# Last state space layer: decay sums from running sums in three bfloat16 parts, one product per unit

## What is computed

```python
def segsum(x):
    """x: (..., T) -> (..., T, T); out[..., i, j] = sum_{j<k<=i} x[..., k]; -inf above diag."""
    ...
def ssd_chunk_scan(X, dA, Bm, Cm, chunk):
    ...
    A = jnp.transpose(dA.reshape(b, c, chunk, h), (0, 3, 1, 2))
    A_cum = jnp.cumsum(A, axis=-1)
    Lm = jnp.exp(segsum(A))
    Y_diag = jnp.einsum('bcshn,bczhn,bhcsz,bczhp->bcshp', Cm, Bm, Lm, X)
...
dt = jax.nn.softplus(A_log)
x_in = x / dt[..., None]
y_ssm = ssd_chunk_scan(x_in * dt[..., None], -dt, Bm, Cm, CHUNK)
```

## Time and profile before

| | us |
|---|---|
| median of 3 runs | 1528.91 |
| lowest and highest | 1528.41 to 1533.25 |
| the profiled execution, its own time | 1531.77 |
| its span, first to last instruction | 1530.0 |
| block `l3a` in it, first `ln` transpose to the last residual | about 1211 to 1434 |
| scan of g = 0, first `cb` to last `o` | about 1266 to 1329 |
| scan of g = 1 | about 1366 to 1433 |

### The profile page before, as it was taken

How to read it: one execution, slowest core, us unless ns; L and a number is a source line. 1 busy time by engine, 2 the same in 40 slices (tenths; PEclk the granted TensorE clock), 3 DMA queues, 4 the chain that set the end, 5 groups by cost and what they waited for, 6 DMA issues and landing times.

```text
span 1530.0 us, 25564 instructions
## 1 busy us (share of the span) xinstructions
PE 1384.1 (90%) x9742; PEld 865.6 (57%) x9760; DVE 912.6 (60%) x1665; ACT 766.3 (50%) x1847; POOL 456.7 (30%) x400
## 2 busy tenths in 40 slices
PE   7869999999899879999999998898997789889799
PEld 3434556555466545666667773665664545545536
DVE  7784322224578654555556688854787587676631
ACT  3452111111777566777776446457776545363230
POOL 3230000000000168786882000120742435314200
PEclk9979999999999999999999999998998898987989
DMA  8020221001200300000000100020001100000000
GB/s 256 28 83 1 67 59 34 1 0 73 92 2 2 125 0 8 7 8 8 8 7 1 76 23 1 1 83 1 2 2 72 56 0 3 3 1 3 30 0 28
DMA packets 21854, 48.12 MB, mean 31 GB/s; under 512 B 1506, under 2 KB 16995, under 8 KB 20580
## 3 DMA queue, kind: packets, MB, share of 16 engines
q1 hardware_dynamic: 21732, 46.47, 8.7%
HBM read 41.22 MB, written 5.24 MB: 30 GB/s over the span
## 4 chain that ended last, share of the span: by engine, by line
PE 68%; DVE 18%; ACT 6%; issue 4%; POOL 4%; DMA 0%; DVEq 0%; ACTq 0%; POOLq 0%
PE PS L862 49%; PE PS L1094 5%; DVE work L2568 5%; PE PS L1153 3%; PE PS L959 3%; PE PS L863 3%; ACT work L1697 2%; PE PS L876 2%; PE PS L1191 2%; DVE small L2040 1%; DVE work L2186 1%; DVE X L2547 1%; DVE work L2536 1%; POOL work L795 1%; PE PS L864 0%
## 5 line engine op out<-in xcount | busy, mean ns | idle before, releaser
L862 PE MATMUL PS<-XT,WB 128*128 128x512 f32 (+1 forms) x688 | 300.5, 595 | 5.1 <-DVE XT L2066 2.8
L862 PEld LDWEIGHTS PS<-XT,WB 128*128 128x128 f32 (+1 forms) x688 | 127.1, 191 | 149.7 <-issue 145.8
L1697 ACT ACTIVATE work<-PS,small 128x128 f32<-128x128 f32 x512 | 137.2, 415 | 45.9 <-DVE small L2371 45.8
L2261 DVE TENSOR_TENSOR work<-PS,work 128x512 f32<-128x512 f32 x48 | 33.1, 691 | 170.1 <-PE PS L862 170.1
L1625 ACT ACTIVATE work<-PS 128x512 f32<-128x512 f32 x48 | 28.7, 597 | 194.6 <-PE PS L862 194.6
L647 POOL TENSOR_SCALAR small<-small 128x4 f32<-128x4 f32 x22 | 5.0, 229 | 402.2 <-DVE small L2043 402.1
L2371 DVE TENSOR_REDUCE small<-PS 128x4 f32<-128x512 f32 x128 | 80.4, 684 | 41.4 <-PE PS L862 40.1
L862 PE MATMUL PS<-XT,WA 128*128 128x512 f32 (+2 forms) x224 | 98.4, 615 | 4.8 <-DVEq L2571 2.5
L2568 DVE SCALAR_TENSOR_TENSOR work<-PS,vec,work 128x508 f32<-128x508 f32 (+2 forms) x108 | 80.2, 742 | 14.3 <-DVE work L2568 7.2
L1094 PE MATMUL PS<-WB,work 128*128 128x256 f32 x384 | 86.9, 379 | 0.5 <-DVE work L2266 0.5
L1094 PEld LDWEIGHTS PS<-WB,work 128*128 128x128 f32 x384 | 72.8, 190 | 18.3 <-issue 7.7
(11 more groups left out here) (377 smaller groups left out, 2860.2 us busy)
## 6 DMA issues: line engine op xcount, KB each, us to landing
WB<-in_l0f SPq DMA_DIRECT2D x8, 768.0 KB, 7.6
WB<-in_l1x SPq DMA_DIRECT2D x1, 6144.0 KB, 19.2
WB<-in_l0f SPq DMA_DIRECT2D x32, 96.0 KB, 6.8
WB<-in_l2f SPq DMA_DIRECT2D x1, 3072.0 KB, 10.2
WA<-in_l3a SPq DMA_DIRECT2D x1, 2624.0 KB, 8.9
WB<-in_l3f SPq DMA_DIRECT2D x1, 2064.0 KB, 7.6
WA<-in_l1f SPq DMA_DIRECT2D x1, 2056.0 KB, 10.0
C<-in_ctx SPq DMA_DIRECT2D x2, 1024.0 KB, 7.0
```

What stands on the lines that cost most here:

```text
L862: mm = lambda o, l, r, s, e: nc.tensor.matmul(o, l, r, start=s, stop=e)
L1697: f(wk(12288 + (u % 8) * G + h * P, P), bank(j)[:, h * P:(h + 1) * P], ACT.Exp, bias=sm(704 + (u % 8) * 4 + h, 1)).then_inc(*act_step(*([j ...
L2261: v.tensor_tensor(l0f_h(m)[:, lo:lo + G], bank(j), l0f_s(m)[:, lo:lo + G], ALU.mult).then_inc(*dve_step(j))
```

## The change

The sums are now taken as differences of running sums. For token i and source j of one head the sum is cum(i) minus cum(j), where cum is the running sum of the steps inside the half. cum is float32; it is split into three bfloat16 parts whose sum is exact, and the difference is one product in bfloat16.

- The `plans()` list gets two new jobs `cum` behind `c` 8 of g = 0. They hold their banks until the third part has been taken.
- TensorE makes cum with 16 small products (`running_sums`), and twice subtracts a part from it (`without_part`), behind `c` 10 and behind `z` 1. ScalarE takes the parts (`split_sums`): after the SiLU of channels 7 and 9, and after the gate of `z` 1, all in g = 0.
- SyncE writes the parts to DRAM (`cum_park`, 6 DMAs) and, for each of the 16 quads, reads them back in 6 DMAs: three of 8 partitions x 4 x 128 elements into the left operand (rows 64 to 87), three of 2 partitions x 32 x 64 elements into the right operand (rows 88 to 93). There are two sets of buffers. The set for quad n is loaded once the last unit of quad n-2 is done.
- The other rows of the two operands are constants: GpSimd writes an identity and a pattern in the block `l2a`, and a pattern after `ln`; VectorE writes the masked rows (`later_tokens`, two instructions of 64 x 2048), one before the copy of `dt` and one after it.
- `seg` is now one bfloat16 product for a unit, 94 rows deep, 128 x 512. GpSimd's 64 tiles (L841) and their waits are gone.
- VectorE waits for the DRAM writes ahead of the fifth unit's scores, and makes two small patterns (32 x 8 and 32 x 2) at the kernel's start.

The core of the diff:

```diff
-        l += [("c", cc, g) for cc in range(12)] + [("z", 4 * g + i) for i in range(4)] + [("ea", g)] + \
+        l += [("c", cc, g) for cc in range(9)] + ([("cum", 0), ("cum", 1)] if g == 0 else []) + \
+            [("c", cc, g) for cc in range(9, 12)] + [("z", 4 * g + i) for i in range(4)] + [("ea", g)] + \
...
+            sp.wait_ge(cum_parts, 6)
+            for g in range(2):
+                for part in range(3):
+                    sp.dma_start(cum_park[part, 4 * g:4 * g + 4].rearrange("b h f z -> h b f z"), cum_part(part)[:, 4 * g:4 * g + 4]).then_inc(cum_parked[g], 16)
+            for n in range(16):
+                b, h0, into = n // 2, 32 * (n % 2), decay_in[n % 2]
+                if n % 8 == 0:
+                    sp.wait_ge(cum_parked[n // 8], 48)
+                if n < 2:
+                    sp.wait_ge(decay_rows, n + 3)
+                    sp.wait_ge(masked_rows, n + 1)
+                else:
+                    sp.wait_ge(*full(J("l3a", "seg", (n - 2) // 8, (n - 2) % 8 * 4 + 3)))
+                for part in range(3):
+                    sp.dma_start(decay_left(...)...).then_inc(into, 16)
+                    sp.dma_start(decay_right(...)...).then_inc(into, 16)
...
-                for u in range(32):
-                    n = 32 * g + u
-                    if n >= 4:
-                        pool.wait_ge(*full(job_of["l3a", "seg", (n - 4) // 32, (n - 4) % 32]))
-                    steps = dt_exchanged[:, n * 8:n * 8 + 8] if n % 2 else wk(14336 + n * 8, 8)
-                    nc.gpsimd.tensor_tensor(r3(l3a_step(n), 64), steps.unsqueeze(2).to_broadcast([P, 8, 64]),
-                                            tri_halves.unsqueeze(1).to_broadcast([P, 8, 64]), ALU.mult).then_inc(half_steps.sem, half_steps.give())
...
+                    if (g, cc) == (0, 8):
+                        running = running_sums()
+                    if (g, cc) == (0, 10):
+                        without_part(running, 0)
...
+                    if (g, cc) == (0, 1):
+                        without_part(running, 1)
...
-                        pair = [(u, begin("l3a", "seg", g, u)) for u in (2 * t, 2 * t + 1)]
-                        for u, o in pair:
-                            pe.wait_ge(half_steps.sem, half_steps.next())
-                            for lo in (0, 64):
-                                at = 64 - lo if u % 2 else lo
-                                ins = mm(o[at:at + 64, :], cst("strict", lo, lo + 64)[:, lo:lo + 64], l3a_step(32 * g + u)[lo:lo + 64, :], True, True)
-                            end(ins, "l3a", "seg", g, u)
+                        for u in (2 * t, 2 * t + 1):
+                            n = 8 * g + u // 4
+                            o = begin("l3a", "seg", g, u)
+                            if u % 4 == 0:
+                                pe.wait_ge(decay_in[n % 2], 96 * (n // 2 + 1))
+                            end(mm(o, decay_left(u % 8)[0:94, :], decay_right(u % 8)[0:94, :], True, True))
...
+            def split_sums(part):
+                for half in range(2):
+                    j = J("l3a", "cum", half)
...
+                    f(cum_part(part)[:, :, half, :], r3(bank(j, 64), 64), ACT.Copy, scale=-1.0).then_inc(cum_parts, 1)
+                    if part == 2:
+                        act.wait_ge(cum_parts, 5 + half)
+                        act.sem_inc(bank_free[bank_of[j]], 1)
...
+                    if g == 0 and cc in (8, 10):
+                        split_sums(cc // 2 - 4)
...
+                    if (g, cc) == (0, 1):
+                        split_sums(2)
```

More of the change, by code:

```diff
@@ L263, in build @@
         identb, causalb, onesb = sb("identb", P, BF16), sb("causalb", 4 * P, BF16), sb("onesb", P, BF16)
-        small = sb("small", 848)
+        small, pattern = sb("small", 848), sb("pattern", 16)
         WORK = 18432
@@ L820, in _ @@
             roots()
-            pool.wait_ge(halves_ready, 2)
-            pool.wait_ge(steps_ready, 1)
[L823 to L827, removed]
+            pool.wait_ge(*full(job_of["l3a", "ln", 1, 1]))
+            for slot in (0, 4):
+                nc.gpsimd.tensor_copy(decay_right(slot, 4)[64:96, :].rearrange("p (u h z) -> p u h z", h=8, z=64),
+                                      by_head.unsqueeze(1).unsqueeze(3).to_broadcast([32, 4, 8, 64])).then_inc(decay_rows, 1)
+                pool.wait_ge(decay_rows, 3 + slot // 4)
+            pool.wait_ge(steps_ready, 1)
             for i in range(4):
@@ L1369, in _, with running_sums, without_part @@
             end(ins)
+            def running_sums():
+                pe.wait_ge(steps_ready, 1)
+                sums = [begin("l3a", "cum", half) for half in range(2)]
+                for half, o in enumerate(sums):
+                    lo = 64 * half
+                    for b in range(NB):
+                        ins = nc.tensor.matmul(o[0:64, b * 64:b * 64 + 64], wk(14336 + b * 64, 64, lo, lo + 64), cst("tri", lo, lo + 64)[:, lo:lo + 64],
+                                               start=b == 0, stop=True, skip_group_check=True)
+                    ins.then_inc(cum_sums, 1)
+                return sums
+            def without_part(sums, part):
+                for half, o in enumerate(sums):
+                    pe.wait_ge(cum_parts, 2 * part + half + 1)
+                    ins = more(r3(o[0:64, :], 64), identb[0:64, 0:64], cum_part(part)[:, :, half, :], True)
+                    if part:
+                        end(ins, "l3a", "cum", half)
+                    else:
+                        ins.then_inc(cum_sums, 1)
             for g in range(2):
@@ L1954, in _ @@
             hidden_evac(6)
+            def split_sums(part):
+                for half in range(2):
+                    j = J("l3a", "cum", half)
+                    if part < 2:
+                        act.wait_ge(cum_sums, 2 * part + half + 1)
+                    else:
+                        act.wait_ge(*full(j))
+                    f(cum_part(part)[:, :, half, :], r3(bank(j, 64), 64), ACT.Copy, scale=-1.0).then_inc(cum_parts, 1)
+                    if part == 2:
+                        act.wait_ge(cum_parts, 5 + half)
+                        act.sem_inc(bank_free[bank_of[j]], 1)
             ln("l3a")
@@ L2096, in masks_and_ones @@
                 v.tensor_copy(onesb[:, :], cst("ones")).then_inc(*dve_step())
+                v.tensor_reduce(by_head, cst("ident", 64, 96).rearrange("p (a c) -> p c a", c=8), AX.X, ALU.add).then_inc(patterns, 1)
+                v.tensor_reduce(by_half, cst("ident", 64, 96).rearrange("p (a c) -> p c a", c=2), AX.X, ALU.add).then_inc(patterns, 1)
                 for i in range(4):
@@ L2686, in _, with later_tokens @@
             raw, dt, rx = wk(13312, 512), wk(14336, 512), wk(14848, 512)
+            def later_tokens(slot):
+                v.tensor_scalar(r3(decay_right(slot, 4)[0:64, :], 64), cst("strict", 0, 64)[:, 0:64].unsqueeze(1).to_broadcast([64, 32, 64]),
+                                NEG, None, ALU.mult).then_inc(masked_rows, 1)
+            later_tokens(0)
             j = J("l3a", "dt")
@@ L2728, in scores @@
                         dve.wait_ge(*full(J("l3a", "yb", g, (u - 8) // 4)))
+                    if (g, u) == (0, 4):
+                        for i in range(2):
+                            dve.wait_ge(cum_parked[i], 48)
                     cbm = l3a_cbm(u % 2)[:, (u % 8 // 2) * 64:(u % 8 // 2 + 1) * 64]
```

35 lines of the change are left out of this document (26 added, 9 removed).

## The result

| | before | after |
|---|---|---|
| median of the runs (20 each), us | 1528.94 | 1532.69 |
| lowest to highest | 1522.86 to 1533.63 | 1528.70 to 1540.51 |
| span of the profiled execution | 1530.0 | 1529.4 |
| ratio, with its 95% interval | | 1.003 (1.0016 to 1.0044) |

What follows compares the result with a forecast made beforehand. VectorE was taken to pace the convolutions, a ScalarE-TensorE-VectorE chain the scan's head, TensorE with waits the scan. Terms -9.2 - 1.3 + 7.8 + 0.3 + 3.0 = +0.6 on 1528.91 gave 1529.5 us, no change; range 1517 to 1546.

Steps and rivals of the forecast that it cites:

- Part 3: Head of the g = 0 scan: `cum` jobs hold two banks, delaying `z` 3, `ea`, `eb` and `x`; +7.8 us.
- rival A: TensorE's low clock stays through the head of the scan: +12.9 to +17 us for +7.8, 1535 to 1539; chance 0.22.
- Part 2: Before each scan: without GpSimd's tiles, VectorE's L2719 falls from 1.95 to 1.3 us; -1.3 us in all.
- Part 1: Scan: shorter `seg` saves TensorE 1.05 us a quad at full clock, partly lost to waits; -9.2 us in all.
- the second quad is free: Octets 2 and 3 of each g: second quad's `seg` saving counts fully, 1.2 us an octet, -4.8 us together.
- Part 4: First octet of g = 0: TensorE idles after the shorter `seg`, so the scan begins at the low clock; +3 us.
- Part 5: DMAs: the parts' writes and each quad's six reads from DRAM stay hidden, by 3 us for later quads; 0.
- rival B: Scan: DRAM reads come late because two-partition copies use few engines; +10 to +25 us, 1540 to 1555; chance 0.13.
- the copies: ScalarE: six copies of 0.6 us each; the first four delay a first tap by at most 0.3 us; +0.3 us.
- Rival C: Scan follows TensorE more than thought: saving 14 to 17 us, 1518 to 1523; chance 0.27 including lesser savings beyond 4.6 us.

Runs made afterwards that it cites:

- e2: Kernel before plus only the running sums, their two banks and the three parts, with no reads and the old `seg`: ratio 1.0047 to before, +7.2 us.
- e1: Changed kernel with all three parts taken one step earlier, so that the `cum` banks are free sooner: ratio 0.9967 to before, median 1525.73 us.
- e3: Changed kernel with each 94-row `seg` product made twice: ratio 1.0039 to before, 1.4 us over after by the ratios.
- e7: Kernel before with only the residual's addition of the output product moved ahead of the C-B products on VectorE: ratio 0.9902 to before.
- e10: e7 with the old `seg` made twice for the last 24 units of each g: ratio 1.0022 to before.
- e12: Kernel before with the whole old `seg` made three times for the first quad of octets 2 and 3 of each g: ratio 1.0033, +5.0 us.
- e8: e1 with the residual added early and the `seg` products of each g's first eight units made three times: ratio 0.9874 to before, 1509.55 us.
- e9: e8 with the `seg` products of the other 48 units made twice: ratio 0.9926 to before.

## Why the prediction came out as it did

The forecast, no change, was right at its edge: +4.6 us measured (2.4 to 6.7) for +0.6, and since the interval leaves out zero, "slightly slower" describes it as well. The mechanisms were mostly as written. One term was mis-sized, the saving in the scan.

- **Part 3 was right.** +7.8 us for the held banks; the rows show +7.3, e2 alone +7.2 us (3.5 to 10.9), and e1 takes it away again. The chain was as counted: gates, copy, `z` 3, `ea`, two `eb` (3.78 for 3.94), `x` (3.58 for 3.68). The clock came back after the pause (0.94 from 1260 to 1265), so that rival A was not so. The masked rows were hidden as counted; they took 2.27 and 1.22 us where I had 2.8 each.
- **Part 2 was right**: L2799 takes 1.23 us in both g instead of 1.95 and 2.05 (1.3 forecast).
- **Part 1, the wait, was right; the sum of it was too large.** The third `y` waits 2.58, 2.58, 2.58 and 2.93 us where 2.7 was forecast, and octet 2 of g = 0 is 1.11 us shorter (1.2 forecast). But the same octet of g = 1 is only 0.18 shorter (17.10 to 16.92). The step that failed is "the second quad is free: 1.05 us at full clock, 2.3 where it was low". I priced the rest of the octet as unchanged, while the wait grew by 0.9 us and what stands behind a longer wait runs at the lower clock longer: the small products 2.05 us against 1.77 before. e3 shows the other side: twice the work, and only 1.4 us more. With the octets 3 (to the last output product of each g: 0.40 shorter in g = 0, 0.44 longer in g = 1) octets 2 and 3 came to -1.25 us together, where I had 4 x -1.2 = -4.8.
- **Part 4 had the right row, and half a reason.** From the first `y` of g = 0 on the clock was 0.50, as the row for 1280 to 1285 shows, and octet 1 grew by 2.3 us. But I put it down to the shorter `seg`, and the traces of e7, e10 and e12 have the old one and the low clock at the same place:

```profile
1279.61 3.09 PE L862 MATMUL PS<-work 64*128 64x128 f32 x16
```

  (timeline of TensorE in e7, second `cb` of g = 0; 1.71 us in the trace of before.) What differs is the execution. In e7 the first `cb` ran at the full clock (1.71 us, before 3.09), and from 1270 to 1275 TensorE was busy for 1.80 us with the old `seg`; in the trace of before, where the clock was still low as the scan began, for 4.15. So an idle stretch did go ahead of the fall, but it doesn't need the shorter `seg`. The full clock in the earlier trace rows was one outcome of several, and counting +3 us for its loss took one profiled execution for the rule.
- **Part 5 was right**: no wait for a read, and rival B was not so. A read mostly took SyncE 0.26 to 0.32 us, not 0.5. The Trainium skill ("DMA: Bandwidth & Descriptors", on why a DMA increments its semaphore by 16) would send the copies of two partitions over two engines; no row here shows how many they used. When they had landed is bounded by e8's first quad, 3.2 us after the last issue; rival B needed over 9 us for the six copies. No run made the reads later, so how far the margin goes is not shown.
- **The sum.** Parts 1, 2 and 4 were -7.5 us together. After against e2 gives -2.6, e1 against before -5.0 (0.6 of it at the head), and the two scans in the profiled executions -1.05 (+0.64 in g = 0, -1.69 in g = 1). Each comes from few executions, but all say that less was saved. With -2.6 the missing 4.9 us, less 0.9 that part 3 and the copies were put too high (8.1 for 7.2), are the difference between +0.6 and the measured +4.6. The scans last 63 and 67 us, 130 together, not the 119 that I wrote beside GpSimd's 70; nothing hangs on it. Rival C (scan follows TensorE) was not so in this kernel, and becomes nearly so once the residual is early.

What I did not see in the profile of before is larger than all of it: a wait that I read as 4 x 1.67 us was worth about 15, and was to be had by moving one call.

## What to carry to other kernels

Before shortening an engine's work, look at the wait that ends the same stretch: as long as the chain over the other engines sets it, the saved time becomes more wait. Price such a wait with the clock of what follows it, not by its own length alone. When a change adds a job to a ring of banks, follow who holds the bank and which jobs stand behind it: two banks held until the second gate cost here more than 64 faster products gave.

## What the runs showed of the hardware

- Moving the residual took away four waits of 1.67 us and gained about 15 us (e7, 9 to 21 by the interval; up to 2.9 of it may be the gaps below). Behind the waits the clock of before fell, as far as 0.66 and 0.73 in the mean of 5 us stretches, and with TensorE kept busy in the same places it stayed at 1.00 (e12, +5.0 us where +10.3 was added net).
- The granted clock at one place differs between executions of nearly the same code: the second `cb` of g = 0 took 1.71 us before and 3.09 us in e7, e10 and e12, which have the same instructions ahead of it in the block. At the first `cb` it is the other way round, 3.09 us before and 1.71 in those three.
- TensorE stood up to 1.9 us in the middle of the small products with nothing that the profile shows to wait for, in all kernels but e9 and e10 (5.1 us in four such gaps in after). Several stand ahead of the same instruction in two executions, with other lengths: ahead of the last 47 records of one `y`, 1.80 us in before and 0.33 in e7; ahead of the last 14 of another, 1.61 in after and 1.28 in e1. I don't know the cause.
- 96 DMAs from DRAM in small pieces (6720 more packets under 512 B) beside the scan made TensorE wait nowhere. Six copies of 8 KB had landed 3.2 us after the last of them began to be issued (e8).
- A VectorE product of 128 x 1024 float32 took 1.95 and 2.05 us beside GpSimd's tiles and 1.23 us without them.
